# Feed forward of a quantized layer: up copies at fixed points of the gate chain, gate's maximum turned one tile earlier, up integers shared anew

## The reference, cut to what matters

```
def act_qdq(x):
    qmax = 2.0 ** (ACT_BITS - 1) - 1.0
    scale = jnp.maximum(jnp.max(jnp.abs(x)) / qmax, 1e-12)
    return jnp.clip(jnp.round(x / scale), -qmax - 1.0, qmax) * scale
...
x = act_qdq(x)
up = act_qdq(x @ lpbq_dequant(w_up).T)
gate = act_qdq(x @ lpbq_dequant(w_gate).T)
sig = fixed_qdq_u16(jax.nn.sigmoid(gate))
gate = act_qdq(gate * sig)
o = act_qdq(gate * up)
return o @ lpbq_dequant(w_down).T
```

## Time and profile before

| | us |
|---|---|
| median of 3 runs | 1288.94 (1288.74 to 1289.71) |
| the profiled execution | 1288.19 |
| its span in the trace | 1286.40 |
| of it, ahead of gate's scale (all of attention, gate's 12 tiles) | 1185.9 |
| the gate chain, to the start of `mine` for ACTED | 32.45 |
| from there to the start of the product phase (line 1663) | 7.94 |
| the product phase, to the start of `mine` for PRODUCT | 18.48 |
| the down product and the end | 41.63 |

### The profile page before, as it was taken

How to read it: one execution, slowest core, us unless ns; L and a number is a source line. 1 busy time by engine, 2 the same in 40 slices (tenths; PEclk the granted TensorE clock), 3 DMA queues, 4 the chain that set the end, 5 groups by cost and what they waited for, 6 DMA issues and landing times. The chain is left out here.

```text
span 1286.4 us, 31443 instructions
## 1 busy us (share of the span) xinstructions
PE 1182.6 (92%) x11707; PEld 919.2 (71%) x11711; DVE 845.0 (66%) x1905; ACT 746.2 (58%) x1330; POOL 879.5 (68%) x750
## 2 busy tenths in 40 slices
PE   5569999999999999999999999999988798879758
PEld 4458888887888888788888888888875566434323
DVE  5857767687777768886676878776655244432762
ACT  3643767676666666666666776666664144513550
POOL 2616988888989888888988888889875133400540
PEclk9879999999999999999999999999999899979879
DMA  5265999999899999999999999999987233860000
GB/s 196 102 191 144 189 205 199 191 191 220 169 214 192 203 190 191 215 175 211 189 203 194 191 194 179 204 201 204 177 168 215 54 99 68 222 161 18 1 0 33
DMA packets 538873, 211.10 MB, mean 164 GB/s; under 512 B 485857, under 2 KB 504289, under 8 KB 538722
## 3 DMA queue, kind: packets, MB, share of 16 engines
q1 hardware_dynamic: 538722, 209.09, 79.8%
HBM read 68.50 MB, written 25.17 MB: 73 GB/s over the span
## 5 line engine op out<-in xcount | busy, mean ns | idle before, releaser
L381 PE MATMUL pair<-arena 128*128 128x256 f16 x2048 | 559.3, 273 | 10.5 <-DVE arena L737 10.5
L383 PE MATMUL pair<-arena 128*128 128x256 f16 x2048 | 559.4, 273 | 0.0
L382 PE MATMUL pair<-arena 128*128 128x256 f16 x2048 | 559.3, 273 | 0.0
L629 POOL TENSOR_TENSOR p_parts<-probs,p_parts 128x512 f16<-128x512 f32 x256 | 306.5, 1205 | 18.0 <-ACT p_parts L699 18.0
L639 POOL TENSOR_TENSOR k_rinv<-k_ms,half_neg 128x8 f32<-128x8 f32 x128 | 225.2, 1760 | 111.5 <-DVE k_ms L784 107.7
L765 DVE CUSTOM_DVE_ANT_0 probs<-bank,mask 128x512 f32<-128x512 f32 x256 | 176.3, 689 | 143.6 <-PE bank L884 140.9
L381 PEld LDWEIGHTS pair<-arena 128*128 128x128 f16 x2048 | 200.2, 98 | 60.8 <-DVE arena L737 10.7
L382 PEld LDWEIGHTS pair<-arena 128*128 128x128 f16 x2048 | 200.3, 98 | 49.9
L383 PEld LDWEIGHTS pair<-arena 128*128 128x128 f16 x2048 | 200.4, 98 | 23.7
L699 ACT ACTIVATE p_parts<-probs 128x512 f16<-128x512 f32 x256 | 161.1, 629 | 94.7 <-DMA pt<-p_parts 76.9
L689 ACT ACTIVATE probs<-probs,neg_max 128x512 f32<-128x512 f32 x256 | 182.9, 714 | 11.4 <-DVE neg_max L774 11.2
(11 more groups left out here) (232 smaller groups left out, 1934.9 us busy)
## 6 DMA issues: line engine op xcount, KB each, us to landing
raws<-in_ctx_t_dram SPq DMA_DIRECT2D x64, 256.0 KB, 3.4
side_kept<-side_parts SPq DMA_DIRECT2D x40, 256.0 KB, 3.6
arena<-side_kept SPq DMA_DIRECT2D x40, 256.0 KB, 4.9
w_kept<-ffn_turned SPq DMA_DIRECT2D x36, 256.0 KB, 3.4
side_raw<-in_w_qkv_dram SPq DMA_DIRECT2D x24, 256.0 KB, 3.4
arena<-w_kept SPq DMA_DIRECT2D x24, 256.0 KB, 4.3
q_kept<-q_st SPq DMA_DIRECT2D x8, 512.0 KB, 2.7
q_now<-q_kept SPq DMA_DIRECT2D x32, 128.0 KB, 3.2
```

What stands on the lines that cost most here:

```text
L381: nc.tensor.matmul(to, x_hi[k], w_hi[k], start=(k == 0), stop=False)
L382: nc.tensor.matmul(to, x_hi[k], w_lo[k], start=False, stop=False)
L383: mm = nc.tensor.matmul(to, x_lo[k], w_hi[k], start=False, stop=(k == n - 1))
L629: nc.gpsimd.tensor_tensor(p_parts[n % PTS][:, 1, :], probs[n % PROBS][:, :], p_parts[n % PTS][:, 0, :], ALU.subtract).then_inc(p_lo_done, 1)
```

## The change

Three things, all in `feed_forward`.

1. A table `KEPT_BY` fixes how many up tiles are copied and reduced by the end of each step of the gate chain. ACT copies tiles 13, 14, 15, 16, 17, 18, 19 in steps 0, 2, 4, 5, 7, 9, 10, and tiles 20 to 23 behind the chain. DVE takes the maxima of tiles 12 to 18 in the same steps, those of 19, 20, 21 between ACTED's `mine` and `one`, those of 22 and 23 behind ACTED's scale.
2. ACTED's column is turned ahead of step 3 of tile 22 (it was step 1 of tile 23) and spread ahead of step 1 of tile 23 (it was step 3).
3. Up's integers: ACT 3, 5, 6, 8, 9, 11 (it was 5, 7, 9, 11); POOL 4, 7, 10 (it was 1, 2, 3, 4, 6, 8, 10); DVE 0, 1, 2 (it was 0). ACTED's integers on ACT are placed around them.

```
-    UP_ACT, UP_POOL = (5, 7, 9, 11), (1, 2, 3, 4, 6, 8, 10)
+    UP_ACT, UP_POOL = (3, 5, 6, 8, 9, 11), (4, 7, 10)
+    KEPT_BY = (13, 13, 14, 14, 15, 16, 16, 17, 17, 18, 19, 19)
...
+                if (m, k) == (2 * KF - 2, 3):
+                    tops_turned(ACTED)
                 if (m, k) == (2 * KF - 1, 1):
-                    tops_turned(ACTED)
-                if (m, k) == (2 * KF - 1, 3):
                     top_spread(ACTED)
...
-                if k + 2 < KF:
-                    kept(KF + 1 + k)
-            kept(2 * KF - 1)
+                for m in range(KEPT_BY[k - 1] + 1 if k else KF + 1, KEPT_BY[k] + 1):
+                    kept(m)
+            for m in range(KEPT_BY[KF - 1] + 1, 2 * KF):
+                kept(m)
...
-                if k < KF - 1:
-                    top_of_raw(KF + k)
+                for m in range(KEPT_BY[k - 1] if k else KF, KEPT_BY[k]):
+                    top_of_raw(m)
                 dve.wait_ge(act_done, k + 1)
                 top(tops[:, 2, k:k + 1], gate_raw[:, k, :], t3_done)
...
+            for m in range(KEPT_BY[KF - 1], 2 * KF - 2):
+                top_of_raw(m)
             top_of_all(ACTED)
             scaled(ACTED, UNIT / QMAX)
             raw_inverse(ACTED, UNIT)
-            top_of_raw(2 * KF - 1)
+            for m in range(2 * KF - 2, 2 * KF):
+                top_of_raw(m)
```

More of the change, by code:

```diff
@@ L1569, in _, with acted_int @@
                 nc.scalar.activation(sig[k % 2][:, :], gate_i[:, k, :], ACT.Sigmoid, scale=scale[:, GATE:GATE + 1]).then_inc(sig_done, 1)
-                if k + 2 < KF:
-                    kept(KF + 1 + k)
-            kept(2 * KF - 1)
-            act.wait_ge(raw_done, 2)
[L1574 to L1579, removed]
+                for m in range(KEPT_BY[k - 1] + 1 if k else KF + 1, KEPT_BY[k] + 1):
+                    kept(m)
+            for m in range(KEPT_BY[KF - 1] + 1, 2 * KF):
+                kept(m)
+            def acted_int(k):
+                nc.scalar.activation(gate_i[:, k, :], gate_raw[:, k, :], ACT.Copy, scale=raw_inv[:, ACTED:ACTED + 1]).then_inc(gi_done, 1)
+            act.wait_ge(raw_done, 2)
+            for k in range(UP_ACT[0] + 1):
+                acted_int(k)
+            act.wait_ge(raw_done, 3)
+            for i, k in enumerate(UP_ACT):
+                nc.scalar.activation(up_i[:, k, :], up_raw[:, k, :], ACT.Copy, scale=raw_inv[:, UP:UP + 1]).then_inc(up_act, 1)
+                for after in range(k + 1, UP_ACT[i + 1] + 1 if i + 1 < len(UP_ACT) else KF):
+                    acted_int(after)
             act.wait_ge(raw_done, 4)
@@ L1663, in _ @@
                     nc.vector.tensor_scalar(up_i[:, k, :], up_raw[:, k, :], raw_inv[:, UP:UP + 1], None, ALU.mult).then_inc(up_dve, 1)
-                    dve.wait_ge(up_dve, 1)
+                    dve.wait_ge(up_dve, k + 1)
                 dve.wait_ge(gi_done, k + 1)
```

## The result

The changed kernel takes 1281.17 us (median of 5 runs, 1279.64 to 1282.76) against 1289.71 for the one before in the same comparison: ratio 0.9939, 95% interval 0.9925 to 0.9953, so faster, by some 0.6%. The profiled execution took 1282.06 us with a span of 1280.3. The forecast was 1282.0 for the median, in a range of 1280.5 to 1284.8. The medians lie 8.5 us apart where the forecast had 6.9; the kernel before was 0.77 slower in this comparison than in the runs that the forecast started from.

The account below looks back on a forecast made before the run. No engine is full in the gate chain; one PE tile, 2.59 us, paces each step. 1288.19 - 6.4 (chain) + 0.45 (PE's turn) - 1.0 (product phase) = 1281.2 us profiled, 1282.0 median; range 1280.5 to 1284.8.

Parts of the forecast that it names:

- The step that carries the forecast: Gate chain: ACT no longer waits for PE's tiles, DVE becomes the bound, ACTED's `mine` comes 6.4 us earlier.
- The mutual slowing: Gate chain: DVE's products and POOL's roundings delay each other, 0.9 us in all, between nothing and 4.1.
- a stall of 1.7 us: PE in tile 22, waiting ahead of step 3 for ACTED's `mine`: 1.7 us in place of 6.71.
- a tail of 5.5: Stretch from ACTED's `mine` to the maximum of tile 23: 5.5 us, where it was 5.00 before.
- The give-back of the earlier turn: PE behind ACTED's turn: 15 matmuls follow it, not 9, giving back 0.45 of the 6.4 us.
- 0.6 in the forecast: PE ahead of ACTED's spread: a further stall of 0.6 us, since `one` comes behind three up maxima on DVE.
- The product phase: First up integer on DVE to PRODUCT's `mine`: 17.5 us, 1.0 less, with no wait for POOL left.
- the mutual slowing of 0.4: Product phase: DVE and POOL delaying each other over POOL's 3 tiles, taken as 0.4 us (nothing to 0.7).
- The end: From PRODUCT's `mine` to the end of the span: unchanged at 41.63 us, with the same half clock at its start.
- A longer stretch at half clock than before: Down product: named as a sign of being wrong, if its half clock lasted longer than in the kernel before.
- The clock did not fall in the new stalls: Rival, chance 0.20: PE's clock falls in its stalls of 1.7 and 0.6 us, costing 1.75 at most: 1283.7 us.
- The rule by which one engine waits out the other's whole instruction: Rival, chance 0.04: in the chain DVE's products never run beside POOL's roundings; `mine` 4.25 us later than forecast: 1286.2.
- scale: Stretch from the maximum of tile 23 to the first up integer on DVE: unchanged at 2.94 us.

Follow-up runs that it names:

- the first experiment: The kernel before with only the new places of the up copies and maxima (KEPT_BY); 1279.73 us median, ratio 0.9923.
- The experiment without the maxima: The changed kernel with the seven maxima of up tiles 12 to 18 moved from the chain to behind ACTED's scale; one execution, 1283.92 us.
- the late turn: The changed kernel with ACTED's column turned ahead of step 1 and spread ahead of step 3 of tile 23; 1279.3 us median, ratio 0.9924.

## Why the prediction was right

**The chain.** The step that carries the forecast held: ACT stopped waiting for tiles, DVE became the bound, 20.67 us where 20.94 was worked out. The copies alone bring it, as the first experiment shows. The mutual slowing was 0.9 in the sum and came out at 0.62: one wait of 0.21, one product at 1.09 and one at 0.82 in place of 0.75. As was argued, DVE falls behind POOL's pace after two steps and most products then start well into POOL's instruction, at 0.74. The experiment without the maxima shows the bound, and how near the next one was: 2.2 us.

**PE's turn.** The forecast was a stall of 1.7 us and a tail of 5.5; it was 1.29 and 5.28. (The 1.7 counts from when the next matmul was due; counted so, the stall was 1.46, the rest of the difference being the shorter chain.) The give-back of the earlier turn was 0.45 in the sum and came out at 0.28 (5.28 less 5.00); that the kernel with the turn left alone would be better by 1.1 us was not seen, because I weighed it against the tail of before and not against this edit left out. The spread waited 0.40 for `one`, behind DVE's three maxima (0.56 counted from when the next matmul was due, 0.6 in the forecast); the same 0.40 stands in all seven kernels whose chain took 20.67 or 20.68.

**The product phase.** This term was mis-sized: 17.5 for 16.81, outside the 17.1 to 17.8 that the prediction named. All three waits for POOL went, as said. But the 0.87 for a tile of integers was taken from a row beside POOL, and the mutual slowing of 0.4 was added on top: counted twice for the first two tiles, and for the third, which starts 0.65 us into POOL's last instruction, not due at all. 3 x 0.87 + 14.4 + 0.1 + 0.4 should have been 0.87 + 0.95 + 0.51 + 14.4 + 0.1 = 16.8.

**The end.** Taken as unchanged, it was 0.56 longer, 42.19. A longer stretch at half clock than before was named as a sign of being wrong, and it came: 3.8 us where the kernel before had 3.4. The change is hardly the cause. PE waited 8.36 us ahead of PRODUCT's turn, 8.45 before, and over all kernels with 44 idle matmuls the end lies between 41.36 and 42.93 without following that wait (8.66 in the shortest, 6.75 in the longest). What sets its length within these bounds stays open.

**The rivals.** The clock did not fall in the new stalls: 1.00 in each microsecond. That is shown for this kernel and not for others: with the late turn it fell by UP's spread, which took 0.55 to 0.58 us in four of the five kernels and 0.38 in the fifth. The rule by which one engine waits out the other's whole instruction gave 1286.2 and is refused by the rows, below. The sum's errors are chain -0.27, tail -0.22, scale -0.05, product -0.69, end +0.56, together -0.67: the longer end hid part of the rest by luck. The profiled execution lay 0.9 above its forecast of 1281.2, since its chain began 1.5 us later, in stages that the change does not touch, and the median lay 0.8 below the forecast. That the absolute times came so close is in part luck too, as these stages move by more than the sum's error.

## What to carry to other kernels

When an engine's list mixes a chain of dependences with a steady job of its own (here copies out of PSUM), the chain runs at the job's pace; give the job to the chain only as often as its buffers need it, and sum up each engine's list to see which bounds next. A duration read beside a busy neighbour already contains what the neighbour costs: look for a row of the same instruction with the neighbour idle before adding a term for it. Where an early step saves one wait, cost it also against leaving that edit out, and look at each stretch by itself when whole runs spread more than the parts.

## What the runs showed of the hardware

**How long POOL holds up DVE.** POOL's three integer tiles in the changed kernel, each 1.56 to 1.60 us:

```profile
1221.17 1.56 POOL L1494 TENSOR_SCALAR up_i<-up_raw,f_raw_inv 128x512 int16<-128x512 f32 x1 [10.77 <-DVE f_raw_inv L1605]
1222.72 1.58 POOL L1494 TENSOR_SCALAR up_i<-up_raw,f_raw_inv 128x512 int16<-128x512 f32 x1
1224.28 1.60 POOL L1494 TENSOR_SCALAR up_i<-up_raw,f_raw_inv 128x512 int16<-128x512 f32 x1
```

DVE's integers beside them, which take 0.48 alone, started 0.13, 0.06 and 0.65 us behind these and took 0.84, 0.92 and 0.48. Less the 0.48, the first two were held until 0.49 and 0.50 us after POOL's start; the third was not held, though POOL's instruction had 0.95 us to go. The product at 1196.33 (0.82, against 0.74 undisturbed) likewise ended inside a rounding, which started at 1196.00: it was held until 0.41 behind that start. So where POOL holds up DVE in these rows, it does so in the first half microsecond of its 1.5, not for the whole of it. The Trainium skill (SBUF — State Buffer, "Who interferes with whom") has the one that comes second blocked for the whole instruction, where the VectorE one has two SBUF inputs, as the product here, or is in a two-port mode, which `tensor_scalar` can enter; here the measurement differs, and it decides. That maxima (TENSOR_REDUCE) are never held agrees with the same section: none in the chain took over 0.69.

**DVE holds up POOL too.** POOL's rounding at 1192.59, which started 0.13 us behind a product, took 1.98 in place of 1.49. And the one that starts second is not always the one that pays. In the kernel before, DVE's product at 1229.84 started 0.05 behind this instruction of POOL and took its usual 0.69, while POOL's took 2.09 in place of 1.56:

```profile
1229.79 2.09 POOL L1493 TENSOR_SCALAR up_i<-up_raw,f_raw_inv 128x512 int16<-128x512 f32 x1
```

Four of POOL's seven up integers took 2.09 or 2.10 there, which lengthened the waits of DVE for POOL that the new shares took away. What decides who pays was not tried.

**How far a single run repeats.** The chain took 20.67 or 20.68 us in seven kernels, while everything ahead of it moved by 5.4 us. The end moved by 1.6 us among the eight kernels that share its instructions. What moves the part ahead of the chain was not looked into.
